# A fused decoder layer: the first batch's cross product moved into the second batch's first attention group, the FFN weights split there, and the tail reordered

## What is computed

```python
x = layernorm(x + attn(x))             # 32 heads of 128, 8 KV heads, rope, causal
x = layernorm(x + fq(x) @ fq(ctx))     # fq: round(x/s + z) clipped to 0..255, minus z, times s
xs, ws = 448 / max|x|, 448 / max|w|
x = layernorm(x + (clip(x * xs) @ clip(w * ws)) / (xs * ws))
# attn(x) = softmax(q k^T) v @ w_o + softmax(q lk^T) lv @ w_lo
#   q, k, v = x w_q, x w_k, x w_v;  lk = (x w_lq) w_lk;  lv = x w_lv
```

## Time and profile before

| | us |
|---|---|
| median of 3 runs | 2589.9 |
| the runs | 2589.59 to 2590.83 |
| span of the profiled execution | 2589.0 |
| PE busy | 2491.2 |
| DVE busy | 1745.9 |
| ACT busy | 1121.6 |
| POOL busy | 871.3 |

### The profile page before, as it was taken

One profiled execution on the slowest core, in us unless ns is written; L12 is line 12 of the kernel. 1 busy time (PEld: TensorE's weight loads), 2 busy tenths in 40 slices (PEclk: granted clock), 3 DMA queues, 4 the chain that ended last, 5 costly groups with the idle time before them and its releaser, 6 DMA issues.

```text
span 2589.0 us, 40621 instructions
## 1 busy us (share of the span) xinstructions
PE 2491.2 (96%) x12544; PEld 2104.0 (81%) x12544; DVE 1745.9 (67%) x3591; ACT 1121.6 (43%) x2552; POOL 871.3 (34%) x654
## 2 busy tenths in 40 slices
PE   8799999999999999999999999999999999998678
PEld 6688888888888888887778888888888888887357
DVE  5676767677676757664766776667676767766964
ACT  3444444353444444353453435444444435343520
POOL 4333342424233332424424242323324242422410
PEclk9999999999999999999999999999999999999889
DMA  5223231313222232313413132322323131325001
GB/s 180 81 70 94 62 98 57 102 55 92 62 77 81 69 93 61 97 53 114 163 55 105 58 92 58 89 71 69 93 61 97 57 102 57 92 63 191 1 17 49
DMA packets 113509, 209.72 MB, mean 81 GB/s; under 512 B 12272, under 2 KB 20592, under 8 KB 113136
## 3 DMA queue, kind: packets, MB, share of 16 engines
q1 hardware_dynamic: 110128, 202.23, 26.3%
q10 hardware_dynamic: 3264, 6.29, 0.7%
HBM read 197.99 MB, written 10.49 MB: 81 GB/s over the span
## 4 chain that ended last, share of the span: by engine, by line
PE 94%; DVE 3%; issue 1%; ACT 1%; POOL 0%; ACTq 0%; DMA 0%; PEldq 0%; POOLq 0%; SPq 0%; DVEq 0%
PE bank_a L979 16%; PE bank_a L981 16%; PE bank_a L980 16%; PE bank_b L979 13%; PE bank_b L980 13%; PE bank_b L981 13%; PE bank_b L1027 5%; DVE probs L651 0%; PE bank_b L1278 0%; PE bank_b L1225 0%; PE bank_a L1246 0%; DVE q L804 0%; PE bank_b L1128 0%; ACT probs L448 0%; DVE stats L879 0%
## 5 line engine op out<-in xcount | busy, mean ns | idle before, releaser
L362 POOL TENSOR_TENSOR w_lo<-w_raw,w_hi 128x512 fp32r<-128x512 f32 x632 | 829.7, 1320 | 1549.4 <-ACT w_hi L411 1538.7
L411 ACT ACTIVATE w_hi<-w_raw 128x512 fp32r<-128x512 f32 x632 | 393.3, 626 | 333.6 <-DMA w_raw<-wstream 131.9
L979 PE MATMUL bank_a<-w_hi,o_hi 128*128 128x512 f32 x1024 | 411.7, 402 | 8.5 <-DVE o_lo L673 5.0
L981 PE MATMUL bank_a<-w_hi,o_lo 128*128 128x512 f32 x1024 | 403.9, 394 | 0.0
L980 PE MATMUL bank_a<-w_lo,o_hi 128*128 128x512 f32 x1024 | 402.8, 393 | 0.0
L668 DVE TENSOR_TENSOR pT_lo<-bank_b,pT_hi 128x512 fp32r<-128x512 f32 (+1 forms) x384 | 207.3, 595 | 269.3 <-ACT pT_hi L454 269.3
L448 ACT ACTIVATE probs<-probs,row_min 128x512 f32<-128x512 f32 (+3 forms) x512 | 281.7, 551 | 232.0 <-DVE row_min L651 232.0
L458 ACT ACTIVATE o_hi<-bank_b 128x512 fp32r<-128x512 f32 x128 | 76.9, 601 | 457.5 <-PE bank_b L981 450.9
L662 DVE TENSOR_SCALAR probs<-probs,row_inv 128x512 f32<-128x512 f32 (+3 forms) x512 | 253.0, 554 | 4.5
L979 PEld LDWEIGHTS bank_a<-w_hi,o_hi 128*128 128x128 f32 x1024 | 194.2, 190 | 43.0 <-DVE o_lo L673 5.4
L981 PEld LDWEIGHTS bank_a<-w_hi,o_lo 128*128 128x128 f32 x1024 | 193.5, 189 | 42.1
(11 more groups left out here) (165 smaller groups left out, 4790.5 us busy)
## 6 DMA issues: line engine op xcount, KB each, us to landing
w_raw<-wstream SPq DMA_DIRECT2D x632, 256.0 KB, 2.7
stage<-ctx SPq DMA_DIRECT2D x32, 256.0 KB, 2.7
q_scratch<-stage_q SPq DMA_DIRECT2D x32, 128.0 KB, 1.7
acc<-x SPq DMA_DIRECT2D x2, 2048.0 KB, 8.8
stage<-wf SPq DMA_DIRECT2D x16, 256.0 KB, 2.7
wf_raw<-wf SPq DMA_DIRECT2D x8, 512.0 KB, 12.8
probs<-xt SPq DMA_DIRECT2D x4, 512.0 KB, 4.1
probs<-xt ACTq DMA_DIRECT2D x4, 512.0 KB, 3.5
```

The lines of the kernel that those rows point to most:

```text
L362: nc.gpsimd.tensor_tensor(w_lo[:, s], w_raw[:, r], w_hi[:, s].bitcast(F32), ALU.subtract).then_inc(lo_done, 1)
L411: nc.scalar.activation(w_hi[:, s], w_raw[:, r], ACT.Copy).then_inc(hi_done, 1)
L979: nc.tensor.matmul(dst, still[0], move[0], start=start, stop=False)
L981: return nc.tensor.matmul(dst, still[1], move[0], start=False, stop=stop)
```

## The change

Batch 0's cross product, residual and its statistics are made in batch 1's first group: x1 is shifted, rounded and centred there (row sums come from ACT's accumulator), `corr0` is added by POOL, and four quarters of the product (`early_cross`) stand in PE's list between output chunks, which are moved back by `NEXT_PARTS`. Rows before the norm go to `r_dram`. Column sums are summed by POOL piece by piece. Both halves of the FFN weights' maximum are taken in batch 0; in batch 1 each group scales, clips and splits two pieces (ACT `piece_high` in slots 29 and 35, POOL `piece_low`) and SP stores them (`store_split`) at c = 34 and at c = 1 of the next group. In the tail FFN is made on unscaled x2 as soon as rows are there; products of batch 0 are parked in SBUF until the scale is known, and PE's order is written out. SP's part:

```diff
+            def store_split(m):
+                sp.wait_ge(piece_lo_done, m + 1)
+                sp.sem_inc(piece_turn, 1)
+                sp.dma_start(wf_hi_dram[m], piece_hi[:].bitcast(F32)).then_inc(wf_out, 16)
+                sp.dma_start(wf_lo_dram[m], stage[:]).then_inc(wf_out, 16)
+            def pieces(b, g, c):
+                G = g + KVH * b
                 if c == 1:
-                    wait(sp, w_part_done, G)
+                    if b == 0:
+                        wait(sp, w_part_done, 2 * G)
+                    elif isinstance(g, int) and g == 0:
+                        sp.wait_ge(w_part_done, 2 * KVH)
+                    else:
+                        store_split(2 * g - 1)
+                        sp.wait_ge(wf_out, 64 * g)
                     sp.sem_inc(piece_turn, 1)
                     sp.dma_start(stage[:], ctxt[2 * G]).then_inc(stage_in, 16)
...
+                if c == 34:
+                    if b == 0:
+                        sp.wait_ge(w_part_done, 2 * G + 1)
+                    else:
+                        store_split(2 * g)
+                        sp.wait_ge(wf_out, 64 * g + 32)
+                    sp.sem_inc(piece_turn, 1)
+                    sp.dma_start(stage[:], wf[2 * g + 1]).then_inc(stage_in, 16)
```

POOL's list (`group`), then ACT's (`crossed`, in batch 1's first group, and the end of each slot):

```diff
+            def group(b, g, first):
+                G = g + KVH * b
+                for c in range(CHUNKS):
+                    low(b, g, c, c)
+                    if c == 12 and first:
+                        wait(pool, colsum_ready, 2 * b)
+                        nc.gpsimd.memset(col_part[:], 0.0).then_inc(cols_added, 1)
+                    if c in (16, 28):
+                        add_columns(b, G, (16, 28).index(c))
+                    if b and first and C_PREV <= c < C_PREV + TT:
+                        add_corr(c - C_PREV, corr0)
+                    if b and c in (33, 37):
+                        piece_low(2 * g + (33, 37).index(c))
...
+            def crossed(c):
+                if c == 3:
+                    load_q2_0()
+                if c == 11:
+                    for t in range(TT):
+                        root_of_x1(0, t)
+                if c in (12, 13):
+                    shift_x1(c - 12)
+                if c in (14, 15):
+                    centre_q1(c - 14)
+                    shift_x1(c - 12)
+                if c in (16, 17):
+                    centre_q1(c - 14)
+                    add_sums(2 * (c - 16))
+                    add_sums(2 * (c - 16) + 1)
+                if c == C_PREV:
+                    for t in range(TT):
+                        copy_q1T(t)
+                if c in (27, 31):
+                    store_r((27, 31).index(c))
+                if c in (29, 33):
+                    load_acc((29, 33).index(c))
...
                     if c == C_PREV:
...
+                        if b and not tg:
+                            crossed(c)
+                            act.wait_ge(corr_added, TT)
                         exponentials(G, 0)
...
                             exponentials(G, u + 2) if u + 2 < UNITS else None
+                        if b and not tg:
+                            crossed(c)
+                        if b and c in (29, 35):
+                            piece_high(2 * g + (29, 35).index(c))
```

DVE's list (in unit u of a group), PE's tables of the first group, and PE's order in the tail:

```diff
+                    if u in (0, 2) and first and b:
+                        for t in range(TT):
+                            cross_residual(t, u // 2)
+                        for t in range(TT):
+                            half_stats_of_r(t, u // 2)
...
-                    if u == 3:
-                        largest_weight(G)
+                    if u in (1, 4):
+                        if b == 0:
+                            largest_weight(G, (1, 4).index(u))
+                        else:
+                            clip_weights(g, (1, 4).index(u))
...
+NEXT_PARTS = [(0, 1), (2, 3), (4, 5), (6,), (7,), (), (), (8,), (9,), (), (10,), (11,), (12,), (13,), (14,), (15,)]
+CROSS_PARTS = {1: (0, 0), 2: (0, 1), 4: (1, 0), 5: (1, 1)}
...
+            for i in range(C_TAIL):
+                output(b, KVH, i, TAIL_POS + i, i, p, 4, lambda t: (added, 4 * (p - 1) + t + 1))
+                if i == 3:
+                    pe.wait_ge(pT_lo_done, 3 * UNITS * KVH * B)
+                    transpose_x2(0)
+                    transpose_x2(1)
+                if i in (5, 6):
+                    transpose_x2(i - 3)
+            ffn(0, 0)
+            ffn(0, 1)
+            pe.wait_ge(x2T_lo_done, 2 * TT)
+            column_sums(1)
+            transpose_q1(TT)
+            transpose_q1(TT + 1)
+            ffn(1, 0)
+            cross_product(0)
+            transpose_q1(TT + 2)
+            cross_product(1)
+            transpose_q1(TT + 3)
+            ffn(1, 1)
+            cross_product(2)
+            cross_product(3)
+            ffn(2, 0)
+            ffn(2, 1)
...
+            for i in range(TT + 2, NT):
+                ffn(i, 0)
+                ffn(i, 1)
```

More of the change, by code:

```diff
@@ L40 @@
 RAW, SPLIT = 4, 6
-CLIPPED_EARLY = 4
 AHEAD = 4
@@ L156, in program, with at @@
[L156 to L162, removed]
+            q1T = sb("q1T", [P, TT, D], BF16, mem)
+        def at(kb, name, shape, dt):
+            with ExitStack() as mem:
+                if kb:
+                    sb(f"ahead_of_{name}", [P, 256 * kb], F32, mem)
+                return sb(name, shape, dt, mem)
@@ L334, in _ @@
+                with sp.Fori(1, last) as g:
                     for c in range(CHUNKS):
                         load(b, g, c, c, chunk(b, 1, c))
-                        pieces(g + KVH * b, c)
-                for c in range(C_TAIL):
-                    load(b, KVH, c, TAIL_POS + c, chunk(b, KVH, c))
+                        pieces(b, g, c)
                 if b + 1 < B:
+                    for c in range(C_TAIL):
+                        load(b, KVH, c, TAIL_POS + c, chunk(b, KVH, c))
                     for c in range(C_LQ):
@@ L506, in group @@
                         shift_piece(G, (8, 19).index(c))
[L507 to L509 removed]
+                    if b and not tg and c < C_PREV:
+                        crossed(c)
                     if 15 <= c < 19:
@@ new lines, in park @@
+            def park(t):
+                act.wait_ge(ffn_ready, 2 * t + 2)
+                for half in range(2):
+                    nc.scalar.activation(product_of(t)[:, N * half:N * (half + 1)],
+                                         BANK_A[2 * (t % 2) + half][:], ACT.Copy).then_inc(ffn_parked, 1)
+            b = B - 1
+            high_ahead(b, KVH, 0, KVH)
+            for i in range(TT):
+                root(i, i)
+            high_ahead(b, KVH, 1, KVH)
+            high_ahead(b, KVH, 2, KVH)
@@ L1126, in group @@
                             pe.wait_ge(consts_in, 64)
+                        if b and first:
+                            pe.wait_ge(corr_done, 2)
                         for t in range(TT):
@@ new lines, in cross_product @@
+            def cross_product(t):
+                i = TT + t
+                pe.wait_ge(q1T_done, i + 1)
+                if t == 0:
+                    pe.wait_ge(q2_in, 16 * (KT // 2))
+                    pe.wait_ge(corr_done, 4)
+                for half in range(2):
+                    if t:
+                        pe.wait_ge(cross_summed, 2 * (i - 1) + half + 1)
+                    for k in range(KT):
+                        last = nc.tensor.matmul(BANK_B[2 + half][:], q1T_1[:, i % 2, P * k:P * (k + 1)],
+                                                q2[:, k, N * half:N * (half + 1)], start=k == 0, stop=k == KT - 1)
+                    last.then_inc(cross_ready, 1)
@@ new lines, in ffn @@
+            def ffn(i, half):
+                pe.wait_ge(x2T_lo_done, 2 * (i + 1))
+                if i == 0 and half == 0:
+                    pe.wait_ge(wf_hi_in, 16 * KT)
+                    pe.wait_ge(wf_lo_in, 16 * KT)
+                if i < 2:
+                    pe.wait_ge(added, 4 * (4 * KVH * B - 1) + 2 * i + half + 1)
+                elif i < TT + 2:
+                    pe.wait_ge(ffn_parked, 2 * (i - 2) + half + 1)
+                else:
+                    pe.wait_ge(ffn_read, 2 * (i - 2 - TT) + half + 1)
+                part = slice(N * half, N * (half + 1))
+                for k in range(KT):
+                    x2 = tuple(x[i // TT][:, i % TT, P * k:P * (k + 1)] for x in (x2T_hi, x2T_lo))
+                    last = product(BANK_A[2 * (i % 2) + half][:], x2, (wf_hi[:, k, part], wf_lo[:, k, part]),
+                                   k == 0, k == KT - 1)
+                last.then_inc(ffn_ready, 1)
```

679 lines of the change are left out of this document (384 added, 295 removed).

## The result

The changed kernel takes 2636.3 us (median of 4 runs, 2634.6 to 2641.6) against 2589.9 us: ratio 1.0181, 95% interval 1.0169 to 1.0193. It is slower, as forecast, by 46 us instead of 57. The profiled execution spans 2632.7 us at a mean clock of 0.978 (before 2589.0, 0.984). One execution of a kernel further down (the second half's residual moved forward) ran at a granted clock of 0.75 and took 3097.4 us; the median given for that kernel leaves it out.

The account below looks back on a forecast made before the run. PE, busy 96% of the span, was taken as the bound. 2589.0 - 69 + 25 + 2 + 52 + 16 + 21 + 10 = 2646, with the 0.9 added 2647 us; range 2598 to 2675.

Parts of the forecast that it names:

- likeliest case: Whole kernel: SP halted at the stores of batch 1's split weights stalls PE; 2620 to 2665 us, chance 0.62.
- Second piece's store, 7.5 a passage: Batch 1, unit 6: SP's store holds back load(2), so PE stalls 7.5 us at seven group passages, 52 us.
- Its clock, 2.3 a stall: Batch 1, after each second-piece stall: idle PE loses clock, charged 2.3 us a stall, 16 in all.
- First piece, 2.6 a group: Batch 1, unit 4's transposes: SP's store holds back load(35), costing 2.6 us in each of eight groups, 21 us.
- First piece's clock, 10 us in all: Batch 1, after each first-piece gap: lost PE clock of 1.3 us in each of eight groups, 10 us.
- rival 2: Batch 1: stalls occur but the clock holds and the first piece is absorbed; 2593, up to 2610 us, chance 0.14.
- Tail, -69: After the last attention product: only batch 1's cross product stays and PE bounds; 125.6 against 195.3 us, bounds -75 to -60.
- allowance of 6 for waits: Tail: PE waits of 6 us, some 2 at the transposes of q1(5) and 4 more spread over the stage.
- x2 transposes inside: Tail: eight FFN tiles at 11.79 us each, 94.3 in all, already containing the transposes of x2.
- First group, +25: Batch 1's first group: longer chains on ACT, POOL and DVE plus added PE work cost 25 us, bounds +12 to +32.
- End of batch 0, +2: End of batch 0: column sums and the wait for pT_lo cost 2 us, the W reduction hidden; bounds 0 to 6.
- Rival 1: Batch 1: stores stay hidden and pieces cost only their ACT and POOL time; 2548 us, chance 0.12.

Follow-up runs that it names:

- kernel of 2545.0: Changed kernel with the first piece's store behind load(37), the second piece's `piece_low` behind chunk 3 and its store behind load(7): 2545.0 us (0.9825).

## Why the prediction was right

Its likeliest case came: the halted SP, at seven passages, decides the sign, and the time of 2636.3 lies inside the range of 2598 to 2675. Point by point, by its steps.

- **Second piece's store, 7.5 a passage: right**, 7.2 in the trace. Every link showed: `piece_high` behind exponentials(7), load(2) behind the landing, pT_high(6) behind the split of chunk 2, ACT waiting 8.15 us for DMA (forecast 8). The store lands in 2.1 to 2.3 instead of 2.4; the removal of the store alone took 3.1 us off the wait, and the move of both took all of it away.
- **Its clock, 2.3 a stall: too small**, 2.9 by the rows of 4 us at one stall, 3.3 by PE's busy time in the mean of the six steady groups.
- **First piece, 2.6 a group: somewhat too large**, 1.85.
- **First piece's clock, 10 us in all: wrong.** The clock stayed at 1.00 behind six of the eight gaps and fell behind two, which is about 3 us by their rows. Here rival 2's remark, that a gap this short doesn't always cost clock, was right. With the item before it 31 was forecast; the move of that store alone gave 21.5 in the median. Its steady groups are 2.2 us shorter each, which makes 18 over eight groups.
- **Steady groups at about 157: right**, 155.9, with those of batch 0 unchanged.
- **Tail, -69: right, somewhat too small.** From the last attention product it took 118.7 instead of the forecast 126: 195.3 - 118.7 = 76.6 saved. That is just outside its bounds of -75 to -60. Two steps failed. One is the allowance of 6 for waits: only the foreseen one, at the transposes of q1(5), came (2.24 us), and PE was full in FFN. The other is "x2 transposes inside": PE's list has those of the first four tiles between the last output chunks (32 from 2500.48 on), ahead of the last attention product, at 0.87 a tile 3.5 us. So 5.1 of the gain are lost again in the last group, 155.8 from its mark to the last attention product instead of 150.7: PE is 3.6 longer busy (148.1 against 144.6), which is these transposes, at the same clock of 0.97, and 1.5 longer idle.
- **First group, +25: about right.** With its share of stalls it was +33.9 against a forecast of 38.7 (25, 7.5, 2.3, 2.6, 1.3); without them the experiment has +21.8. Unit 0's values were 11.2 later, of a forecast 13. The mechanism, chains and not PE's work, stands by the experiment with a quarter of the product. The two halves of 5.2 on DVE met PE as predicted at `own(0)`, 5.41, and little elsewhere.
- **End of batch 0, +2: failed.** It took +5.9. The step said that the W all-reduce falls where POOL's splits lead PE by about 9 us, and priced it by its own short duration. POOL was away 7.24 us before it and 7.27 after it, more than the lead, and PE stood 2.17. The 7.1 us of the first pause was in a row of the kernel before. With the reduction replaced by a copy the stretch is 186.6, +1.8 against before, PE's idle time is that of before (5.4), and the +2 forecast for the column sums is right. The other 4.1 are the reduction's.

By the marks, forecast against measured: end of batch 0 +2 and +5.9, first group +38.7 and +33.9, six steady groups +82 and +73.6, the rest -65 and -71.5, start 0 and +1.7. Every part has its sign right. The total was 11 us high. Too high were above all the first piece (some 7 in its clock, 6 in its length), the first group and the tail's waits (4); the end of batch 0 (4) and the clock behind the second piece's stall (some 6 over seven) were too low and hid part of it. By that luck the total is nearer than its terms.

**Rival 1**, the stores hidden, was priced at 2548. The change as it was given didn't take that road, but the same work in another order did, at 2545.0. The fault and the gain were independent, as the sum had them.

## What to carry to other kernels

A queue that both prefetches and waits is as late as its slowest wait: before a wait goes into it, list what stands behind it and which engine's next instruction needs that, then put the wait behind as many prefetches as the buffers hold. Two positions in SP's list turned a change of +46 us into one of -34, and one in POOL's, with the store behind it, made it -45. Where the bounding engine idles because of chains on others, count what is added to the chains: its own added work filled the gaps here.

## What the runs showed of the hardware

- A partition all-reduce on POOL took 0.58 us, with 7.24 us of pause before it and 7.27 before the next ordinary instruction (7.20 and 6.67 in the kernel of 2545.0); with a copy of 0.19 us in its place there was neither pause. The Trainium skill (GPSIMD Engine Reference, "Instruction dispatch") gives about 6 us for the first call of a freshly loaded kernel, with no instruction visible; here the pause came on the way back as well. That both are code loading is only argued.
- Four f32 passes of DVE over 128x512 to 128x128 took 1.27 us with POOL idle, 1.94 beside 0.87 us of POOL's two-input operations, 2.96 beside about 2.3, and 4.20 beside POOL working throughout.
- 7.2 us of PE idleness brought the clock to 0.50 until 3 to 6 us after work began again, at the three of the seven stalls that were read (at 1547.02, 1703.14 and 1858.18). Gaps of 1.59 to 1.85 us left it at 1.00; one of 1.94 and one of 2.49 did not, while one of 1.96 did again (at 1801.43, with only the second piece's store moved).
